# Attention's row transposes split by block, tables loaded in two steps, residual transfers moved to ScalarE's queue

## The reference

```python
x = x + attn_a(layernorm(x))      # one row's value, broadcast over the sequence
x = x + ffn(layernorm(x))         # RWKV-like feed-forward
x = x + attn_b(layernorm(x))      # 16 heads of 64, window of 128
x = x + ffn(layernorm(x))
```

```python
q = rope(x @ Wq.T + bq); k = rope(x @ Wk.T + bk); v = x @ Wv.T + bv
# each block of 128 queries sees its own block of keys and the one before, masked to a band
attn = softmax(where(valid, q @ kcat.T / 8, -1e30))
out = (attn @ vcat) @ Wo.T + bo
```

## Time and profile before

| | us |
|---|---|
| median of 3 runs | 1627.13 |
| lowest, highest | 1625.92, 1627.72 |
| profiled execution, its time | 1629.63 |
| its span | 1627.8 |
| granted TensorE clock, mean | 0.979 |

### The profile page before, as it was taken

The page is one execution under the profiler, slowest core; times in us unless marked ns, Lnnn a source line. Parts: engine busy times, 40 slices in busy tenths (PEclk is TensorE's granted clock), DMA queues, the critical chain, the costliest instruction groups (busy, mean ns, idle before and its releaser), DMA issues. The chain is left out here.

```text
span 1627.8 us, 46830 instructions
## 1 busy us (share of the span) xinstructions
PE 1503.2 (92%) x16866; PEld 1145.2 (70%) x16866; DVE 1403.6 (86%) x3859; ACT 1324.8 (81%) x2442; POOL 1137.7 (70%) x911
## 2 busy tenths in 40 slices
PE   5999878899999999999999999999999999869998
PEld 4888745576767676666767676767676767658887
DVE  5999668899989999999999898999898889857885
ACT  5999658888878888888888787888788878749996
POOL 4665367778777887878788777787787777623443
PEclk7999989999999999999999999999999999979999
DMA  5242247889998999999998999899989998962331
GB/s 210 92 124 99 65 100 128 169 164 176 169 183 159 176 161 184 165 187 170 170 184 157 172 166 169 168 176 172 173 151 175 165 166 159 172 157 69 109 111 70
DMA packets 728445, 247.92 MB, mean 152 GB/s; under 512 B 688148, under 2 KB 715032, under 8 KB 728216
## 3 DMA queue, kind: packets, MB, share of 16 engines
q1 hardware_dynamic: 727512, 244.53, 78.1%
q10 hardware_dynamic: 704, 0.40, 0.1%
HBM read 47.73 MB, written 25.17 MB: 45 GB/s over the span
## 5 line engine op out<-in xcount | busy, mean ns | idle before, releaser
L1283 DVE CUSTOM_DVE_ANT_0 at_prob<-banks,at_masks,pre_s_scale 128x256 f32<-128x256 f32 (+1 forms) x1024 | 421.3, 472 | 25.8 <-PE banks L1697 9.3
L1446 ACT ACTIVATE at_prob<-at_prob,at_top 128x256 f32<-128x256 f32 (+1 forms) x1024 | 428.3, 490 | 16.5 <-DVE at_top L1283 14.1
L1295 DVE TENSOR_TENSOR at_halves<-at_prob,at_halves 128x1024 f16<-128x1024 f32 (+1 forms) x256 | 331.7, 1296 | 3.1 <-ACT at_halves L1455 3.1
L1582 PE MATMUL banks<-at_xt,pre_w_h 128*128 128x512 f16 x1024 | 299.4, 385 | 12.4 <-ACT at_v_l L1474 7.6
L1697 PE MATMUL banks<-at_kt,at_qt 32*128 32x256 f32 (+1 forms) x4096 | 253.4, 384 | 31.5 <-issue 20.8
L1455 ACT ACTIVATE at_halves<-at_prob 128x1024 f16<-128x1024 f32 (+1 forms) x256 | 263.4, 1029 | 6.1
L1697 PEld LDWEIGHTS banks<-at_kt,at_qt 32*128 32x128 f32 x4096 | 198.6, 187 | 93.1 <-issue 88.4
L1653 PE MATMUL banks<-at_v_h,at_pt 128*128 128x65 f16 x1984 | 208.9, 195 | 32.7 <-DMA at_pt<-at_halves 25.8
L1653 PEld LDWEIGHTS banks<-at_v_h,at_pt 128*128 128x128 f16 x1984 | 182.1, 98 | 73.2 <-DMA at_pt<-at_halves 41.0
L1175 POOL TENSOR_TENSOR at_kt<-at_k_by 128x512 f32<-128x512 f32 x128 | 171.5, 1340 | 77.3 <-DVE at_halves L1295 65.6
L1165 POOL TENSOR_TENSOR at_q_by<-at_q_first,at_tables 128x512 f32<-128x512 f32 x128 | 175.5, 1375 | 61.5 <-DVE at_halves L1295 60.8
(11 more groups left out here) (123 smaller groups left out, 3319.1 us busy)
## 6 DMA issues: line engine op xcount, KB each, us to landing
f_x<-in_x SPq DMA_DIRECT2D x16, 512.0 KB, 3.7
x_after_ffn<-f_x SPq DMA_DIRECT2D x16, 512.0 KB, 2.7
at_x_res<-x_after_ffn SPq DMA_DIRECT2D x64, 128.0 KB, 3.1
x_after_attention<-at_x_res SPq DMA_DIRECT2D x64, 128.0 KB, 2.7
f_x<-x_after_attention SPq DMA_DIRECT2D x16, 512.0 KB, 4.4
out_x<-f_x SPq DMA_DIRECT2D x16, 512.0 KB, 3.0
at_x_ln<-x_after_ffn SPq DMA_DIRECT2D x32, 128.0 KB, 3.2
at_tables<-in_cos SPq DMA_DIRECT2D x16, 256.0 KB, 4.0
```

The source lines that it names most:

```text
L1283: last = nc.vector.tensor_tensor_reduce(out=prob[:, n % 2, h, low:2 * P], in0=s_ps[:, h, n % 2 * 2 * P + low:(n % 2 + 1) * 2 * P], in1=mas ...
L1295: nc.vector.tensor_tensor(parts[:, 1, :, :], prob[:, n % 2, :, keys_from(t, b):2 * P], parts[:, 0, :, :], ALU.subtract).then_inc(p_low, 1)
L1446: last = nc.scalar.activation(at, at, ACT.Exp, bias=top[:, n % 2, h:h + 1], scale=-1.0)
L1582: last = nc.tensor.matmul(pr_ps[:, half, :].rearrange("p (b t) -> p b t", b=SB), w[wp][:, k, at:at + P], xt[:, r, xp, :, k, :], start=n == ...
```

## The change

1. `turn_x` takes a block n instead of a superblock: x_halves and xt get the block as the outer index, and each step t issues the transpose of block t+6 after `turn_p(t, 2)`. The first superblock is still turned by one DMA (`first_turn_x`, at t = -4). It waits for the low half of the block, for the former block's transpose, and for the values of the superblock that used the buffer.
2. The high half of block n waits for the transpose of block n-4 alone.
3. `load_tables` becomes `load_table(S, e)`: cosine at g = 3, two superblocks ahead, sine at g = 1, one ahead.
4. Residual load and store are issued by ScalarE, after `context_high(t - 1)`; from t = 64 on by SyncE. Row t-3 is loaded instead of t-4.
5. Row loads at the seam: blocks 4 to 7 at t = -8 to -6, blocks 8 to 10 at t = -3, that is after the last stores of ffn1 (before: 4 and 5 at -8, then one a step).

```diff
@@ attention_stage
-    x_halves = sb("x_halves", [P, 2, SB, C], F16)
-    xt = sb("xt", [P, 2, 2, SB, CK, P], F16)
+    x_halves = sb("x_halves", [P, SB, 2, C], F16)
+    xt = sb("xt", [P, 2, SB, 2, CK, P], F16)
...
+    LOADED = {-8: (4, 5), -7: (6,), -6: (7,), -5: (), -4: (), -3: (8, 9, 10)}
...
+    def xt_turned(n):
+        S, blk = divmod(n, SB)
+        return 16 * (SB * (S // 2) + blk + 1) if S % 2 else 16 * (1 + SB * (S // 2 - 1) + blk + 1) if S else 16
     def xt_ready(S):
-        return 16 * (S // 2 + 1)
+        return xt_turned(SB * S + SB - 1)
@@ sync
-        def turn_x(S):
-            if big(S):
-                sp.wait_ge(x_low, SB * (S + 1))
+        def first_turn_x():
+            sp.wait_ge(x_low, SB)
+            sp.wait_ge(past.moved[0], past.stores(2 * past.SLOTS))
+            sp.dma_start(xt[:, 0, :, :, :, :].rearrange("p b e k t -> p (b e k) t"),
+                         x_halves[:, :, :, :].rearrange("p b e c -> p (b e c)"),
+                         transpose=True).then_inc(xt_in[0], 16)
+
+        def turn_x(n):
+            if step(n):
+                S, blk = divmod(n, SB)
+                sp.wait_ge(x_low, n + 1)
+                sp.wait_ge(xt_in[(n - 1) // SB % 2], xt_turned(n - 1))
                 need(v_done[1], NG * (S - 1))
-                if S < 2:
-                    sp.wait_ge(past.moved[S], past.stores(S + 2 * past.SLOTS))
-                sp.dma_start(xt[:, S % 2, :, :, :, :].rearrange("p e b k t -> p (e b k) t"),
-                             x_halves[:, :, :, :].rearrange("p e b c -> p (e b c)"),
+                if n == SB:
+                    sp.wait_ge(past.moved[1], past.stores(1 + 2 * past.SLOTS))
+                sp.dma_start(xt[:, S % 2, blk, :, :, :].rearrange("p e k t -> p (e k) t"),
+                             x_halves[:, blk, :, :].rearrange("p e c -> p (e c)"),
                              transpose=True).then_inc(xt_in[S % 2], 16)
...
-        def load_tables(S):
+        def load_table(S, e):
...
-                for e, table in enumerate((cos, sin)):
-                    sp.dma_start(tables[:, S % 2, e, :], table[:, at:at + SB * P]).then_inc(tab_in[S % 2], 16)
+                sp.dma_start(tables[:, S % 2, e, :], (cos, sin)[e][:, at:at + SB * P]).then_inc(tab_in[S % 2], 16)
...
         def at_step(t):
             S, g = divmod(t, NG)
             turn_p(t - 1, 3)
-            if g == 0:
-                turn_x(S + 1)
+            if t == -4:
+                first_turn_x()
             turn_context(t - 2)
             turn_p(t, 0)
-            load_residual(t - 4)
-            store(t - 6)
-            if g == 0 and S >= 0:
-                load_tables(S + 1)
             turn_p(t, 1)
             turn_p(t, 2)
-            if t == -8:
-                load_x(SB)
-            load_x(t + 13)
+            if t + 6 >= SB:
+                turn_x(t + 6)
+            if t >= STEPS:
+                load_residual(t - 3)
+                store(t - 6)
+            for n in LOADED.get(t, (t + 13,)):
+                load_x(n)
+            if g == 3 and S >= -1:
+                load_table(S + 2, 0)
+            if g == 1 and S >= 0:
+                load_table(S + 1, 1)
@@ scalar
                 act.wait_ge(xn_made, n + 1)
-                need(xt_in[(S - 1) % 2], xt_ready(S - 1))
+                if S > 0:
+                    act.wait_ge(xt_in[(S - 1) % 2], xt_turned(n - SB))
...
+        def load_residual(i):
+            if step(i):
+                need(stored[i % RB], 16 * (i // RB))
+                if i < RB:
+                    act.wait_ge(past.low_made, 2 * past.CHUNKS)
+                act.dma_start(x_res[:, i % RB, :], x_in[:, i, :]).then_inc(res_in[i % RB], 16)
+
+        def store(i):
+            if step(i):
+                act.wait_ge(x_made, i + 1)
+                act.dma_start(x_out[:, i, :], x_res[:, i % RB, :]).then_inc(stored[i % RB], 16)
...
             context_high(t - 1)
+            store(t - 6)
+            load_residual(t - 3)
             if t + 8 >= SB:
                 normalize(t + 8)
                 x_high_of(t + 8)
```

More of the change, by code:

```diff
@@ L1122, in opening @@
                 load_x(n)
-            load_tables(0)
+            load_table(0, 0)
+            load_table(0, 1)
             sp.dma_start(bv_cols[:, :], bv).then_inc(const_in, 16)
@@ L1201, in x_low_of @@
                 pool.wait_ge(x_high, n + 1)
-                nc.gpsimd.tensor_tensor(x_halves[:, 1, blk, :], x_ln[S % 2][:, blk, :], x_halves[:, 0, blk, :],
+                nc.gpsimd.tensor_tensor(x_halves[:, blk, 1, :], x_ln[S % 2][:, blk, :], x_halves[:, blk, 0, :],
                                         ALU.subtract).then_inc(x_low, 1)
@@ L1336, in x_low_of @@
                 dve.wait_ge(x_high, n + 1)
-                nc.vector.tensor_tensor(x_halves[:, 1, blk, :], x_ln[S % 2][:, blk, :], x_halves[:, 0, blk, :],
+                nc.vector.tensor_tensor(x_halves[:, blk, 1, :], x_ln[S % 2][:, blk, :], x_halves[:, blk, 0, :],
                                         ALU.subtract).then_inc(x_low, 1)
@@ L1528, in x_high_of @@
                 act.wait_ge(xn_made, n + 1)
-                need(xt_in[(S - 1) % 2], xt_ready(S - 1))
+                if S > 0:
+                    act.wait_ge(xt_in[(S - 1) % 2], xt_turned(n - SB))
                 if S == 0:
                     act.wait_ge(past.moved[5], past.stores(11))
-                nc.scalar.activation(x_halves[:, 0, blk, :], x_ln[S % 2][:, blk, :], ACT.Copy).then_inc(x_high, 1)
+                nc.scalar.activation(x_halves[:, blk, 0, :], x_ln[S % 2][:, blk, :], ACT.Copy).then_inc(x_high, 1)
+        def load_residual(i):
[8 more added lines that the diff above has]
+                act.dma_start(x_out[:, i, :], x_res[:, i % RB, :]).then_inc(stored[i % RB], 16)
         def first_rows():
@@ L1582, in project @@
                     last = nc.tensor.matmul(pr_ps[:, half, :].rearrange("p (b t) -> p b t", b=SB),
-                                            w[wp][:, k, at:at + P], xt[:, r, xp, :, k, :],
+                                            w[wp][:, k, at:at + P], xt[:, r, :, xp, k, :],
                                             start=n == 0 and k == 0, stop=n == 2 and k == CK - 1)
@@ L1599, in values @@
                             last = nc.tensor.matmul(
-                                pr_ps[:, half, blk * 2 * P:(blk + 1) * 2 * P], xt[:, r, xp, 2 * half + blk, k, :],
+                                pr_ps[:, half, blk * 2 * P:(blk + 1) * 2 * P], xt[:, r, 2 * half + blk, xp, k, :],
                                 w[wp][:, k, VC + g * 2 * P:VC + (g + 1) * 2 * P],
```

## The result

The changed kernel takes 1608.23 us (1604.13 to 1608.56, 4 runs) beside 1626.53 for the kernel before (1624.18 to 1627.72, 4 runs); the ratio is 0.9878, with a 95% interval from 0.9865 to 0.989. Measured once more beside the experiments it was 0.987 (0.9854 to 0.9886). The gain is 1.2 to 1.3%, 18 to 21 us; 34 were forecast. The direction and the range held, the size did not: 1608 lies outside the forecast's own band (1587 to 1602), in the part of the range that was added for a partial gain.

What follows compares the result with a forecast made beforehand. The prediction took TensorE's pace (18.4 us a step) as the bound, with SyncE's DMA backlog lengthening 14 second steps. 1627.1 - 35.3 + 3 - 2.5 = 1592.3, stated as 1592.5 us; range 1586 to 1618.

Steps and rivals of the forecast that it cites:

- The bound: Attention steps: TensorE's own pace sets 18.4 us; DMA backlog on SyncE's queue lengthens each superblock's second step.
- The long steps' saving: Attention stage: 14 long second steps fall from 292.3 to 257.0 us, saving 35.3.
- the control: Superblock 15, without rows to transpose or tables to load: second step 18.42 us, taken as the pace without backlog.
- Given back: Attention steps: 3 us lost, 0.05 a step, for quarter transposes now in every step; bounds 0 and 19.
- The sign named for these transposes: Changed kernel's attention steps: TensorE would have no wait of over 0.5 us for a probability transpose.
- A quarter's issue: SyncE's queue: issuing a quarter row transpose takes 0.8 us; 0.5 to 0.9 if by size, 1.23 with a floor.
- ScalarE's two DMAs: ScalarE, each step: issuing residual load and store takes 0.9 us, hidden under 2.4 to 3.4 us of cover.
- The second rival: ScalarE's DMAs wait for SyncE's transposes, holding it 4.5 us a step: 1656 us; chance 0.12.
- The first rival: DMA engines are the limit, all steps 18.8 us: 1608.5; chance 0.20, shared with a partial gain.
- the sentence behind it: Long steps: the same 1608.5 us comes out if half the excess belongs to something the change leaves in place.
- The seam: Before attention: later row loads free the first row transpose, VectorE's key products start 2.5 us earlier; bounds 0 and 2.8.
- The sum: Whole kernel: 1627.1 - 35.3 + 3 - 2.5 = 1592.3 us, stated as 1592.5.

Runs made afterwards that it cites:

- e7: Kernel before with only the row transposes by block (and the high half's earlier release); ratio to the kernel before 0.9909, 58 steps 1081.69 us.
- e9: Kernel before with only the two table loads put into two different steps; ratio to the kernel before 0.9903, 58 steps 1084.03 us.
- e1: Changed kernel with POOL's inverse deviation moved ahead of its wait for block 3's low half; 1602.7 us, ratio to the kernel before 0.9856.
- e2: Changed kernel with the power of POOL's inverse deviation computed a second time into a spare tile; ratio to the kernel before 0.9959.
- e6: Changed kernel with POOL's inverse deviation and its input double buffered and computed one step earlier; ratio to the kernel before 0.9818.
- e11: Kernel before with only POOL's inverse deviation double buffered and a step earlier; ratio to the kernel before 1.0017.
- e4: Changed kernel with residual load and store back on SyncE's queue; 1605.1 us, ratio to the kernel before 0.9871.
- e10: Changed kernel with the seam's row loads of blocks 6 to 10 at their old steps; ratio to the kernel before 0.9885.

## Why the prediction was right or wrong

**The bound.** Right: a normal step is 18.4 us, TensorE's own pace, before and after, and the DMA backlog behind row transpose and tables made the long steps longer. e7 and e9 show it from two sides. Wrong is the sentence that nothing on TensorE waits for a probability transpose in a normal step: in nine of the first steps before, the matmuls wait 0.7 to 1.7 us for one, and seven of the nine take 18.4 to 18.5, as that of superblock 2 does without such a wait. So some two fifths of the 22.9 us of such waits cost nothing, or nearly, and the total is no measure of the gain.

**The long steps' saving, 35.3 us.** This is the term that failed. 14 long steps fell from 292.3 to 270.9 us, 21.4, not 35.3. The step that failed is the control: I took superblock 15 for a superblock without row transpose and tables, and set the whole excess over 18.36 down to the DMA queue. But superblock 15 also lacks the inverse deviation on POOL, and so does superblock 14. The row that would have told was in my own table: the second step of superblock 14 took 20.63, so without the deviation the DMA backlog alone was 2.2 us there. What the deviation alone makes of a step could be seen in superblocks 4 and 8, where the step was near 19.1 and where the change altered next to nothing (19.06 and 19.21 before, 19.05 in both after). The remainder after the change is 13 steps of about 1.07 us, 14 us, and e1, e2 and e6 show whose it is. The excesses didn't add before; the later of the two set the step's end (e11). So after taking away one, the other showed in full. Superblock 14, the better control, isn't a pure one either (it has no rows to load and normalize); that the rest is the deviation's is shown by e6, not by it.

**Given back, 3 us.** The 44 other steps took 809.3 instead of 807.9: 1.4. Within its bounds, but not for the reason given: e4 and e7 have the quarters too, and their 44 other steps take 807.8. The 1.4 stand only in the kernels that have the quarters and the residual transfers on ScalarE's queue together; why isn't known. The sign named for these transposes failed by little: the matmuls' longest wait for one is 0.8 us, not under 0.5.

**A quarter's issue, 0.8 us.** It is longer. Issue durations in the changed kernel, ns min/median/max: the row transposes, then ScalarE's store and residual load. They answer to the earlier trace rows.

```profile
L1095 SPq DMA_TRANSPOSE at_xt<-at_x_halves x60: 1195/1208/1931, 201.7 to 1297.7; - x60
...
L1566 ACTq DMA_DIRECT2D x_after_attention<-at_x_res x58: 326/326/331, 344.0 to 1403.7; - x58
...
L1560 ACTq DMA_DIRECT2D at_x_res<-x_after_ffn x61: 326/445/1312, 286.3 to 1404.1; - x61
```

The quarter takes 1.21, near the 1.23 of the shortest probability transposes, which are those of a sequence's first block and half the size. So issue doesn't follow size: the upper of my two bounds. It cost nothing, since SyncE had the time.

**ScalarE's two DMAs, 0.9 us, hidden.** The store is issued 0.9 to 1.7 us before L1513 even starts, under the arithmetic ahead of it. The wait before the key copy is 116.9 us in 49 steps, 2.39 each, as before (2.40); I had forecast 1.5 to 2. The time was not even taken from the cover.

```profile
475.17 0.60 ACT L1493 ACTIVATE at_v_l<-banks 128x512 f16<-128x512 f32 x1
475.57 0.33 ACTq L1566 DMA_DIRECT2D x_after_attention<-at_x_res  x1
475.66 0.59 ACT L1493 ACTIVATE at_v_l<-banks 128x512 f16<-128x512 f32 x1
475.94 0.73 ACTq L1560 DMA_DIRECT2D at_x_res<-x_after_ffn  x1
```

The second rival (ScalarE held by SyncE's transposes) is refuted. 14 of the 61 residual loads and three of the 58 stores began while SyncE was issuing a transpose; for the 14, 1.8 to 3.0 us of it were left, and they took 0.36 to 0.45 us. One of them:

```profile
530.71 2.99 SPq L1067 DMA_TRANSPOSE at_pt<-at_halves  x1
530.77 0.44 ACTq L1560 DMA_DIRECT2D at_x_res<-x_after_ffn  x1
```

The two loads near 1.3 us weren't among them. The rule of the Trainium skill on which it rested, in "Perfetto Trace Analysis", section "DMA Instruction — HWDGE (DVE, Sync)", has a lock wait inside the reported duration; no wait of a transpose's length shows in these 14, and the measurement decides.

**The first rival** (DMA engines at their limit, the work only spreads, 1608.5 us) named the measured time almost to the microsecond and is wrong as a mechanism: normal steps stayed at 18.42, not 18.8, and e6 went below it with the same transfers. What fits is the sentence behind it, that part of the excess belongs to something the change leaves in place; I had not named the something.

**The seam, 2.5 us.** Right at its place: 2.7 by e10 against the repeated run. VectorE's first key product came at 202.79 instead of the forecast 206, because the three loads were issued from 197.91, not 200.5; the first stage ended 2.4 us earlier in that execution. Half of the gain was lost in the next steps.

**The sum.** 1626.53 less 20.0 in the steps and less about 1.4 at the seam is 1605; measured were 1608.23 and 1604.71. What is left over, 0 to 3 us, is within what one execution of this kernel differs from another.

## What to carry to other kernels

A stretch where the suspect is absent is a control only if nothing else is absent there too: list all that runs once per period, on every engine, before the whole excess is given to one of them. Where two delays fall into the same step, the later one sets its end; removing it uncovers the other, and removing the other first gives nothing (e11 against e6). Before a work item is cut into pieces, look for what else lies in the same step: moving one of two neighbours (the tables, 16.2 us) gave nearly as much as cutting up the other (18.5), while a third delay hid what each left.

## What the runs showed of the hardware that was not expected

- The issue of a DMA transpose didn't shrink with its size below a half: 1.20 us at the least for a quarter, 1.23 for a half, and 1.64 for the shortest whole one of the probabilities (before). The median of the whole row transposes was 2.81 us.
- Two probability transposes in a row took 5.3 to 5.5 us of issue behind the two residual DMAs and 6.6 without them, in steps with no backlog: 1 us of issue taken off the queue came back in what followed.
- ScalarE's sequencer issued a store of 128 KB in 0.33 us and a load in 0.45 (medians; the longest load 1.31) while its arithmetic went on; two a step left no trace in its waits.
- POOL and VectorE slowed each other when certain operations overlapped: VectorE's low half went from 1.21 to 2.21 us beside POOL's key product, POOL's 128x4 addition from 0.20 to 1.29 beside VectorE's low half, and POOL's bias from 0.72 to 1.63 beside the same. A shift of 1 us between the two engines cost 1 us a superblock (e1). Which of the operands' paths they share wasn't tried.
